# Steps 0 and 1 of a transformer tower in another order: maxima, exponentials and outputs ahead of the projections' work

## The chip, the cores and the metric

The kernel runs on one core of one Trainium2 chip. The metric is device time in microseconds (us), the median of repeated runs of the whole program. The core has five engines with their own instruction streams: PE (matrix products), DVE (vector), ACT (activation functions), POOL (GpSimd) and SP (which issues DMAs here). They meet only at semaphores, so what an engine does next is fixed by the order in which the program was written.

## The reference

It takes 16 sequences of 128 tokens and a width of 256. Cut to what matters:

```python
h = layernorm(word_emb[ids] + pos_emb + type_emb[types]) * gamma + beta
a = layernorm(h)
q, k, v = a @ Wq, a @ Wk, a @ Wv              # 16 heads of 16
q, k = layernorm(q) * qw + qb, layernorm(k) * kw + kb   # per head
h = h + softmax(causal(q @ k.T / 4)) @ v @ Wo + bo
s = softmax(layernorm(h) @ gate.T)            # 8 experts, best 2 by s + bias
h = h + sum over the 2: (silu(x w1) * (x w3)) @ w2,  x = s * layernorm(h)
```

## The kernel before, in words

The program has an attention stage, a short routing stage and an expert stage of 39 tiles of 128 rows. The change and the prediction concern the beginning of the attention stage.

**Attention** handles one sequence per step, in a software pipeline. Each engine has its own function `step(t, p, half)`, and `attention` calls it for t = -5 to 17: -5 to 2 written out, 3 to 10 in a loop of two steps, the rest written out. `valid(t)` is true for 0 to 15, and `at_step(t, n)` is true only in a step that is written out and has number n. In step t a sequence is at these places:

- Sequence t + 5: POOL gathers its word rows (`gather`, L426) and, from sequence 5 on, prepares position and type rows (L535 to L537, called x_base below).
- Sequence t + 4: DVE adds them (`sum_rows`, L888 and L892, with statistics in L775 and L776), centers them (`centered`, L899), applies the first layer norm (`first_norm`, L905) and takes statistics for the second (`stats`). POOL turns variances into reciprocal roots (`power_e`, `power_a`, L430 and L431).
- Sequence t + 3: DVE applies the second norm (`normalize_a`, L779), and POOL adds the output bias into the residual (`output_bias`, L471).
- Sequence t + 2: PE transposes the normalized rows (L1129), ACT copies them out of PSUM (L670), PE projects them to q and k (`project`, L1243), ACT squares these (`squares`, L664), DVE sums the squares per head (`squared_sums`, L862 to L865), POOL finds the reciprocal roots by ten small operations (`qk_power`, L437 to L447), and DVE multiplies (`normalize_qk`, L878).
- Sequence t + 1: PE transposes q and k (L1129), ACT copies them out with scale and bias (`queries_and_keys_out`, L657), and PE projects v (`values`).
- Sequence t: PE computes the scores (`scores`, L1202) into PSUM banks 0 to 3, into which `mask_bank` (L1194) has put the causal mask. DVE takes row maxima, one instruction per bank (`maxima`, L856). ACT takes the exponentials, four instructions per bank (`exponentials`, L620). PE transposes them (`keys_to_rows`, L1129), into the bank they came from, or into T_BANK for the last, and ACT copies the result to SBUF (`transposed`, L627).
- Sequence t - 1: PE multiplies probabilities and values (`outputs`, L1219), and ACT, PE and DVE bring the result back to rows, divide it by the sums (L983, L984) and multiply it by Wo (L1342).

T_BANK is one PSUM bank, used in turn by the transposed q and k and by the last of the four transposed banks of probabilities. The columns q and k of the next sequence must be copied out before `keys_to_rows(3)` may write there.

**Order around the change.** In the steps ahead of 0 the pipeline fills. In step 0 PE computes the scores of sequence 0, runs 14 matmuls of no use (`keep_warm`, L1137, here into T_BANK), and only then goes on. ACT takes two banks of exponentials, then copies q and k, then comes the rest. DVE takes `sum_rows(3)` and `centered(3)` at the end of step -1, then the maxima, and `normalize_qk(2)` at the end of step 0. POOL runs `power_e(4)` ahead of `qk_power(2)`. All of it waits in order: whatever stands behind a waiting instruction on an engine waits too.

At the start of the program PE runs `keep_warm(WARM_START)`, 32 matmuls of no use, until the first normalized rows are there; another 14 (`WARM_FIRST`) stand in step -1.

Of the kernel before, what the change touches and what calls it, by code (L numbers as in the profile page):

```python
# [9 lines left out]
B = 16  # L10
# [22 lines left out]
WARM_START, WARM_FIRST, WARM_EXPERTS = 32, 14, 16  # L33
# [17 lines left out]
def build_tower(nc, ids, types, word, rows, w_qkv, w_o, head_cols, gate_t, w1, w3, w2, out):  # L51
# [7 lines left out]
    with ctx:  # L59
# [311 lines left out]
        def _(pool):  # L371
# [77 lines left out]
            def step(t, p, half):  # L449
# [47 lines left out]
                else:  # L497
# [23 lines left out]
                    if valid(t + 5):  # L521
                        gather(t + 5, 1 - p, link)
                    if valid(t + 4):
                        power_e(t + 4)
                    if at_step(t, B - 3):
                        hot_cells(0, 0, 4)
                    if valid(t + 2):
                        qk_power(t + 2, link)
# [72 lines left out]
        def _(act):  # L601
# [12 lines left out]
            def step(t, p, half):  # L614
# [52 lines left out]
                if valid(u):  # L667
                    act.wait_ge(aT_ps, u + 1)
                    wait(act, v_done, u - 1)
                    a.activation(aT[p].rearrange("p k s -> p (k s)"), PS[:, O_BANK, 0:D],  # L670
                                 ACT.Copy).then_inc(aT_ready, 1)
                if valid(t):
                    exponentials(0)
                    exponentials(1)
# [72 lines left out]
        def _(dve):  # L747
# [102 lines left out]
            def step(t, p, half):  # L850
# [79 lines left out]
                elif at_step(t, -1):  # L930
                    normalize_a(2)
                    squared_sums(1)
                    sum_rows(3, 1, 1)
                    centered(3, 1)
# [5 lines left out]
                if at_step(t, 0):  # L940
                    normalize_qk(1)
                    first_norm(3)
                    stats(link, row(3), 1, var_a)
                if at_step(t, B):
                    one_hots(1, (1,))
                if at_step(t, B + 1):
                    places(2, link)
                if valid(t + 4) and valid(t):
                    sum_rows(t + 4, p, half(4))
                u = t - 2  # L950
# [35 lines left out]
                if valid(t + 2) and valid(t):  # L986
                    squared_sums(t + 2)
# [6 lines left out]
                if valid(t + 4) and valid(t):  # L994
                    first_norm(t + 4)
# [7 lines left out]
                if valid(t + 4) and valid(t):  # L1003
# [32 lines left out]
                if valid(t + 2) and valid(t):  # L1036
# [87 lines left out]
        def _(pe):  # L1124
# [55 lines left out]
            def step(t, p, half):  # L1180
# [93 lines left out]
                if at_step(t, 0):  # L1274
                    keep_warm(WARM_FIRST, T_BANK)
                u = t + 2
                if valid(u):
# [4 lines left out]
                    transposes(a_n, DK, O_BANK).then_inc(aT_ps, 1)  # L1282
                u = t + 1
# [6 lines left out]
                if valid(t - 1):  # L1290
# [12 lines left out]
                if valid(t):  # L1303
# [8 lines left out]
                if valid(t) and not at_step(t, B - 1):  # L1312
# [19 lines left out]
                if valid(t):  # L1332
# [133 lines left out]
```

## Time and profile before

| | us |
|---|---|
| median of 3 runs | 551.74 (550.8 to 553.6) |
| the profiled execution's own time | 551.53 |
| its span, first to last instruction | 549.8 |
| mean granted clock of PE in it | 0.986 of full |
| PE busy | 512.2 (93% of the span) |
| DVE, ACT, POOL busy | 285.3, 258.0, 287.2 |

The span is divided so: scores of sequence 0 start at 29.3 us, scores of sequence 15 at 200.5 us, the first expert tile's products at 232.8 us. "Busy" of an engine is time with an instruction in execution, and "idle before <-" in a row names the work that ended the idle time ahead of it. "PEclk" is the granted share of PE's full clock: 1.00 is 2.4 GHz, 0.50 is 1.2 GHz. In the timeline of PE, one matmul in the program is often two instructions, and the time of a row reaches to the end of its last one, so the next row can start up to 0.17 us before that.

### The profile page before, as it was taken

What the parts mean: (1) busy time and instruction counts of PE and PEld (TensorE: products, weight loads), DVE (VectorE), ACT (ScalarE), POOL (GpSimd) and SP (SyncE); (2) the same over time, 40 slices, a digit from 0 to 9 for tenths busy, and PEclk for the clock granted to TensorE, in tenths of its full rate; (3) what the DMA queues carried; (4) which work ended last, traced back from release to release, by engine and by line L of the source; (5) the groups of instructions that cost most, each with busy time, mean ns of one, the idle gap of its engine ahead of it and who ended that gap; (6) DMA issues with size and microseconds to landing.
All of it is one profiled execution on the core that took longest, in us unless ns stands there. A gap on an engine that the chain in (4) does not pass through costs nothing.

```text
span 549.8 us, 12957 instructions
## 1 busy us (share of the span) xinstructions
PE 512.2 (93%) x4263; PEld 432.1 (79%) x4264; DVE 285.3 (52%) x743; ACT 258.0 (47%) x591; POOL 287.2 (52%) x532
## 2 busy tenths in 40 slices
PE   6788999999999998799999999999999999999991
PEld 2345767777676765399999999999999999999981
DVE  3786888878888887723333333333333333333330
ACT  1068888988999784142333233322333223332320
POOL 4587787677754565215334544454434544454432
PEclk9899999999999999989999999999999999999996
DMA  5017611100028672401122212221122212222221
GB/s 164 10 44 270 211 49 44 44 29 29 29 76 275 212 239 81 100 20 26 36 39 39 30 28 39 39 39 23 36 39 39 33 26 38 39 34 31 32 39 19
DMA packets 29482, 36.64 MB, mean 67 GB/s; under 512 B 7792, under 2 KB 23024, under 8 KB 29456
## 3 DMA queue, kind: packets, MB, share of 16 engines
q0 software_dynamic: 8352, 12.76, 13.7%
q1 hardware_dynamic: 20288, 22.51, 12.9%
q10 hardware_dynamic: 816, 1.06, 0.6%
q8 instruction: 13, 0.21, 0.2%
q14 instruction: 13, 0.11, 0.1%
HBM read 26.81 MB, written 9.50 MB: 66 GB/s over the span
## 4 chain that ended last, share of the span: by engine, by line
PE 80%; POOL 5%; DVE 4%; ACT 4%; issue 3%; DMA 2%; SPq 0%; DVEq 0%; ACTq 0%; POOLq 0%
PE PS L1391 35%; PE PS L1402 18%; PE PS L1129 9%; PE PS L1243 6%; PE PS L1342 3%; PE PS L1202 2%; PE PS L1219 2%; PE PS L1194 2%; DMA cols_sb<-head_cols_dram 1%; ACT work L620 1%; PE PS L1256 1%; DMA out_dram<-x_pair,dst_c 1%; PE PS L1137 1%; POOL arena L471 1%; DVE ss L862 0%
## 5 line engine op out<-in xcount | busy, mean ns | idle before, releaser
L1391 PEld LDWEIGHTS PS<-work,arena 128*128 128x128 f32 x1716 | 199.2, 194 | 3.8 <-ACT work L724 2.0
L1391 PE MATMUL PS<-work,arena 128*128 128x128 f32 x1716 | 199.8, 277 | 1.5 <-ACT work L724 1.5
L730 ACT ACTIVATE work<-PS 128x768 f32<-128x768 f32 x39 | 31.6, 810 | 198.9 <-PE PS L1391 198.9
L1402 PE MATMUL PS<-w_sb,work 128*128 x468 | 107.6, 380 | 0.7 <-DVE x_pair L1104 0.7
L1096 DVE TENSOR_TENSOR work<-work,PS 128x640 f32<-128x640 f32 x39 | 32.0, 821 | 139.5 <-ACT work L730 139.5
L1402 PEld LDWEIGHTS PS<-w_sb,work 128*128 128x128 f32 x468 | 86.1, 191 | 11.0 <-issue 1.1
L564 POOL DMA_INDIRECT out_dram<-x_pair,dst_c x39 | 80.5, 2065 | 22.0 <-POOL dst_c L563 20.5
L563 POOL COPY dst_c<-dest_i 128x1 int32 (+1 forms) x39 | 7.1, 181 | 136.5 <-DVE x_pair L1104 134.3
L620 ACT ACTIVATE work<-PS,nmax 128x128 f32<-128x128 f32 x256 | 72.6, 404 | 4.7 <-DVE nmax L856 4.7
L720 ACT ACTIVATE arena<-w_sb 128x1408 f32 x40 | 55.1, 1377 | 13.9 <-DVE er_i L1072 8.9
L1129 PE MATMUL PS<-ident,work 128*128 128x128 f32 x336 | 55.4, 278 | 2.8 <-ACT work L620 1.4
L1129 PEld LDWEIGHTS PS<-ident,work 128*128 128x128 f32 x336 | 38.7, 141 | 19.8 <-ACT work L620 10.8
L1243 PE MATMUL PS<-w_sb,front 128*128 128x512 f32 (+1 forms) x128 | 48.9, 506 | 0.6 <-ACT front L670 0.6
L1082 DVE COPY arena<-w_sb 128x1408 f32 x40 | 36.0, 900 | 25.8 <-issue 25.8
L557 POOL DMA_INDIRECT work<-x_rows,src_c x39 | 39.7, 1018 | 10.8 <-POOL src_c L556 10.8
L627 ACT ACTIVATE work<-PS 128x512 f32<-128x512 f32 x64 | 42.0, 656 | 0.3 <-PE PS L1129 0.3
L856 DVE TENSOR_REDUCE nmax<-PS 128x4 f32<-128x512 f32 x64 | 39.7, 683 | 2.0 <-PE PS L1202 1.6
L1104 DVE COPY x_pair<-PS 128x256 f32<-128x256 f32 x39 | 16.6, 425 | 36.9 <-PE PS L1402 36.9
L1137 PE MATMUL PS<-identb 128*128 128x512 bf16 x115 | 29.2, 403 | 5.3 <-POOL identb L390 5.3
L556 POOL COPY src_c<-src_i 128x1 int32 (+1 forms) x39 | 29.6, 759 | 7.5 <-PE PS L1129 7.5
L1129 PE MATMUL PS<-ident,arena 128*128 128x128 f32 x160 | 25.8, 276 | 6.2 <-DVE arena L878 4.4
L1243 PEld LDWEIGHTS PS<-w_sb,front 128*128 128x128 f32 x128 | 22.0, 191 | 11.8 <-issue 10.1
(165 smaller groups left out, 621.9 us busy)
## 6 DMA issues: line engine op xcount, KB each, us to landing
w_sb<-w_dram SPq DMA_DIRECT2D x16, 640.0 KB, 6.2
w_sb<-w_dram SPq DMA_DIRECT2D x8, 704.0 KB, 4.5
x_rows<-x SPq DMA_DIRECT2D x16, 128.0 KB, 2.2
out_dram<-arena SPq DMA_DIRECT2D x16, 128.0 KB, 2.3
w_sb<-w_dram SPq DMA_DIRECT2D x16, 64.0 KB, 6.5
w_sb<-w_qkv_dram ACTq DMA_DIRECT2D x1, 768.0 KB, 8.0
work<-x_rows,src_c POOLq DMA_INDIRECT x41, 2.9
out_dram<-x_pair,dst_c POOLq DMA_INDIRECT x39, 4.2
```

What stands on the lines that cost most here:

```text
L557: g.indirect_dma_start(xg_sb[p], None, x2_dram, bass.IndirectOffsetOnAxis(src_c[p][:, :], 0)).then_inc(xg_loaded[p], 16)
L564: g.indirect_dma_start(out, bass.IndirectOffsetOnAxis(dst_c[p][:, :], 0), y_sb[p][:, :], None, compute_op=ALU.add).then_inc(y_stored[p], 16)
L620: last = a.activation(probs[:, c * P:(c + 1) * P], PS[:, r, g * P:(g + 1) * P], ACT.Exp, bias=nmax[:, c:c + 1])
L627: a.activation(probsT[:, r * 512:(r + 1) * 512], PS[:, T_BANK if r == RG - 1 else r, :], ACT.Copy).then_inc(probsT_ready, 1)
L720: a.activation(ws[p][:, 0:1, :], w13_sb[:, bass.ds(e, 1), 0, :], ACT.Copy).then_inc(w_a_ready, 1)
L856: v.tensor_reduce(nmax[:, RG * r:RG * r + RG], PS[:, r, :].rearrange("p (g s) -> p g s", s=P), axis=AX.X, op=ALU.max, negate=True).then_in ...
L1082: v.tensor_copy(ws[p][:, 1:2, :], w13_sb[:, bass.ds(e, 1), 1, :]).then_inc(w_v_ready, 1)
L1129: last = n.transpose(PS[:, bank, at + i * P:at + (i + 1) * P], src[:, i * P:(i + 1) * P], ident[:, :])
L1137: n.matmul(PS[:, bank, :], identb[:, :], spread(identb[:, :], 1, GROUPS), start=True, stop=True)
L1243: last = n.matmul(PS[:, bank, 0:w], a[:, k, :], wqkv_sb[:, k, w0:w0 + w], start=(k == 0), stop=(k == DK - 1))
L1391: last = n.matmul(up_ps[p][:, i, c, :], ws[p][:, k, at:at + P], xT_sb[p][:, k, :], start=(k == 0), stop=(k == DK - 1))
L1402: last = n.matmul(PS[:, 7, 0:D], hT_sb[p][:, i, :], w2_sb[:, bass.ds(e, 1), i, :], start=(i == 0), stop=(i == FK - 1))
```

## The change

Nothing is added to or taken from what is computed. The order of steps 0 and 1 is changed on four engines, and the number of useless matmuls in two places:

- PE: `WARM_START` is 42 instead of 32. In step 0 the 14 useless matmuls become 7, and stand behind the transposes of sequence 2's rows instead of ahead of them. `keys_to_rows(0)`, `(1)` and `(2)` of step 0 come ahead of the transposes of q and k. In step 1 `outputs(0)` comes ahead of the transposes of q and k.
- ACT: in step 0 all four exponentials come first, then two copies of probabilities, then q and k, then the rest.
- DVE: the maxima of step 0 come ahead of `sum_rows(3)` and `centered(3)`, with `normalize_qk(1)` between these two. `first_norm(4)`, its statistics and `normalize_qk(2)` move from step 0 to behind the maxima of step 1. `squared_sums(2)` moves ahead of `centered(4)`.
- POOL: `qk_power(2)` comes ahead of `power_e(4)`.

```diff
-WARM_START, WARM_FIRST, WARM_EXPERTS = 32, 14, 16
+WARM_START, WARM_FIRST, WARM_EXPERTS = 42, 14, 16
...
+                    if at_step(t, 0):
+                        qk_power(2, link)
                     if valid(t + 4):
                         power_e(t + 4)
                     if at_step(t, B - 3):
                         hot_cells(0, 0, 4)
-                    if valid(t + 2):
+                    if valid(t + 2) and not at_step(t, 0):
                         qk_power(t + 2, link)
...
+                if at_step(t, 0):
+                    for r in range(RG):
+                        exponentials(r)
+                    transposed(0)
+                    transposed(1)
+                    queries_and_keys_out(1)
+                    transposed(2)
+                    squares(2)
+                    values_out(1)
+                    transposed(3)
+                    return
...
                     squared_sums(1)
-                    sum_rows(3, 1, 1)
-                    centered(3, 1)
                 if valid(t):
                     maxima(0)
...
                 if at_step(t, 0):
+                    sum_rows(3, 1, 1)
                     normalize_qk(1)
+                    centered(3, 1)
                     first_norm(3)
                     stats(link, row(3), 1, var_a)
...
+                if at_step(t, 1):
+                    normalize_qk(2)
+                    first_norm(4)
+                    stats(link, row(4), 1, var_a)
                 if valid(t + 4) and valid(t):
                     sum_rows(t + 4, p, half(4))
+                if at_step(t, 0):
+                    squared_sums(2)
...
-                if at_step(t, 0):
-                    keep_warm(WARM_FIRST, T_BANK)
                 u = t + 2
                 if valid(u):
...
                     transposes(a_n, DK, O_BANK).then_inc(aT_ps, 1)
+                if at_step(t, 0):
+                    keep_warm(WARM_FIRST // 2, T_BANK)
+                    keys_to_rows(0)
+                    keys_to_rows(1)
+                    keys_to_rows(2)
+                if at_step(t, 1):
+                    outputs(0)
```

The calls that these replace get `and not at_step(t, 0)` (or 1) in their old places.

On PE, the stretch from the scores of sequence 0 to the last mask product of step 0 (`ident,work` rows are `keys_to_rows`, `ident,front` the transposes of normalized rows, `ident,arena` those of q and k, `w_sb,front` projections, 512 columns wide for q and k, 256 for v) stood so before:

```order
L1202 MATMUL PS<-w_sb 128x128 x16
L1137 MATMUL PS<-identb 128x512 x14
L1129 MATMUL PS<-ident,front 128x128 x2
L1129 MATMUL PS<-ident,arena 128x128 x4
L1243 MATMUL PS<-w_sb,front 128x512 x2
L1129 MATMUL PS<-ident,work 128x128 x8
L1243 MATMUL PS<-w_sb,front 128x256 x2
L1194 MATMUL PS<-mask,identb 128x512
L1129 MATMUL PS<-ident,work 128x128 x4
L1194 MATMUL PS<-mask,identb 128x512
L1129 MATMUL PS<-ident,work 128x128 x4
L1194 MATMUL PS<-mask,identb 128x512 x2
```

and stands so now:

```order
L1221 MATMUL PS<-w_sb 128x128 x16
L1148 MATMUL PS<-ident,front 128x128 x2
L1156 MATMUL PS<-identb 128x512 x7
L1148 MATMUL PS<-ident,work 128x128 x12
L1148 MATMUL PS<-ident,arena 128x128 x4
L1262 MATMUL PS<-w_sb,front 128x512 x2
L1262 MATMUL PS<-w_sb,front 128x256 x2
L1213 MATMUL PS<-mask,identb 128x512 x2
L1148 MATMUL PS<-ident,work 128x128 x4
L1213 MATMUL PS<-mask,identb 128x512 x2
L1221 MATMUL PS<-w_sb 128x128 x16
```

The useless matmuls (`identb` alone) are half as many and one place later. Twelve of the sixteen transposes of probabilities have moved from behind the projection of q and k to ahead of the transposes of q and k.

On DVE, the stretch from the end of step -1 to the statistics of sequence 3 in step 0 (`nmax` are the maxima, `arena<-PS,rqk` is `normalize_qk`, the rows from `rows_sb,typesf` to `mv<-st` are `sum_rows`, and `L269 ISA` clears a semaphore at the end of a step) stood so before:

```order
L888 SCALAR_TENSOR_TENSOR front<-rows_sb,typesf 128x256
L892 TENSOR_TENSOR x_pair<-x_pair,front 128x256
L775 BN_STATS st<-x_pair 128x6
L776 BN_AGGR mv<-st 128x2
L899 SCALAR_TENSOR_TENSOR front<-x_pair,mv,rows_sb 128x256
L269 ISA
L856 TENSOR_REDUCE nmax<-PS 128x4 x4
L878 TENSOR_TENSOR arena<-PS,rqk 128x512
L905 SCALAR_TENSOR_TENSOR arena<-front,rstd,rows_sb 128x256
L775 BN_STATS st<-arena 128x6
L776 BN_AGGR mv<-st 128x2
```

and stands so now:

```order
L269 ISA
L869 TENSOR_REDUCE nmax<-PS 128x4 x4
L901 SCALAR_TENSOR_TENSOR front<-rows_sb,typesf 128x256
L905 TENSOR_TENSOR x_pair<-x_pair,front 128x256
L788 BN_STATS st<-x_pair 128x6
L789 BN_AGGR mv<-st 128x2
L891 TENSOR_TENSOR arena<-PS,rqk 128x512
L912 SCALAR_TENSOR_TENSOR front<-x_pair,mv,rows_sb 128x256
L918 SCALAR_TENSOR_TENSOR arena<-front,rstd,rows_sb 128x256
L788 BN_STATS st<-arena 128x6
L789 BN_AGGR mv<-st 128x2
```

The maxima have moved ahead of the four instructions of `sum_rows(3)`, and `centered(3)` (L899, L912 now) to behind `normalize_qk(1)`.

## Rows read from the trace of the kernel before

**Rows 1.** the page, section 4: the chain that ended last, shares of the span
```profile
PE 80%; POOL 5%; DVE 4%; ACT 4%; issue 3%; DMA 2%; SPq 0%; DVEq 0%; ACTq 0%; POOLq 0%
```

**Rows 2.** windows, one step each: length, busy by engine, granted clock, DMA share, GB/s
```profile
29.30:43.37 14.07, 10.75 (x82) 6.41 (x81) 12.39 (x29) 9.49 (x28) 11.81 (x29) 1.00 0.31 103
...
55.51:66.59 11.08, 10.84 (x115) 7.95 (x114) 8.93 (x24) 9.77 (x30) 8.07 (x21) 1.00 0.54 175
```

**Rows 3.** timeline of PE: start us, us, engine, line, operation, [idle before <-releaser]
```profile
5.31 8.58 PE L1137 MATMUL PS<-identb 128*128 128x512 bf16 x32 [5.31 <-POOL identb L390]
...
17.73 2.94 PE L1243 MATMUL PS<-w_sb,front 128*128 128x512 f32 x4 [0.56 <-ACT front L670]
...
20.46 3.97 PE L1137 MATMUL PS<-identb 128*128 128x512 bf16 x14
...
27.49 1.88 PE L1243 MATMUL PS<-w_sb,front 128*128 128x512 f32 x4
...
30.41 3.20 PE L1137 MATMUL PS<-identb 128*128 128x512 bf16 x14
```

**Rows 4.** windows, clock after the warm start, and two stretches of little PE work
```profile
19.00:20.00 1.00, 1.00 (x2) 0.50 0.13 49
...
13.89:17.73 3.84, 0.41 (x3) 0.21 (x3) 3.63 (x10) 0.38 (x1) 2.50 (x4) 1.00 0.00 0
...
33.82:36.75 2.93, 0.50 (x5) 0.50 (x5) 2.93 (x5) 2.44 (x9) 2.60 (x8) 1.00 0.00 0
```

**Rows 5.** timeline of DVE, from the first squared sums to step 1
```profile
21.33 0.69 DVE L862 TENSOR_REDUCE ss<-w_sb 128x32 f32<-128x512 f32 x1 [0.93 <-ACT w_sb L664]
...
31.07 0.48 DVE L888 SCALAR_TENSOR_TENSOR front<-rows_sb,typesf 128x256 f32<-128x256 f32 x1
...
33.12 2.48 DVE L856 TENSOR_REDUCE nmax<-PS 128x4 f32<-128x512 f32 x4
...
35.51 0.68 DVE L878 TENSOR_TENSOR arena<-PS,rqk 128x512 f32<-128x512 f32 x1
...
45.91 2.48 DVE L856 TENSOR_REDUCE nmax<-PS 128x4 f32<-128x512 f32 x4
```

**Rows 6.** timeline of ACT, step 1: exponentials
```profile
46.62 2.17 ACT L620 ACTIVATE work<-PS,nmax 128x128 f32<-128x128 f32 x8 [1.29 <-DVE nmax L856]
```

**Rows 7.** timeline of PE, steps 0, 1 and 2
```profile
36.25 0.66 PE L1129 MATMUL PS<-ident,arena 128*128 128x128 f32 x4 [2.43 <-DVE arena L878]
...
36.75 1.88 PE L1243 MATMUL PS<-w_sb,front 128*128 128x512 f32 x4
...
42.35 0.66 PE L1129 MATMUL PS<-ident,work 128*128 128x128 f32 x4 [0.64 <-ACT work L620]
...
46.05 0.66 PE L1129 MATMUL PS<-ident,arena 128*128 128x128 f32 x4 [1.14 <-DVE arena L878]
...
56.89 0.60 PE L1129 MATMUL PS<-ident,arena 128*128 128x128 f32 x4
```

**Rows 8.** timeline of POOL, steps -1 to 1
```profile
34.95 0.19 POOL L430 TENSOR_TENSOR veps<-mv,eps 128x1 f32<-128x1 f32 x1
...
35.76 2.27 POOL L471 TENSOR_TENSOR arena<-arena,rows_sb 128x256 f32<-128x256 f32 x3
...
37.99 0.37 POOL L430 TENSOR_TENSOR veps<-mv,eps 128x1 f32<-128x1 f32 x1
...
41.79 0.23 POOL L437 TENSOR_TENSOR nwt<-guess 128x32 f32<-128x32 f32 x1
...
47.20 0.73 POOL L537 TENSOR_TENSOR front<-front,rows_sb 128x256 f32<-128x256 f32 x1
...
52.37 0.41 POOL L437 TENSOR_TENSOR nwt<-guess 128x32 f32<-128x32 f32 x1 [1.26 <-DVE guess L865]
...
55.65 0.25 POOL L447 TENSOR_TENSOR rqk<-nwt 128x32 f32<-128x32 f32 x1
```

**Rows 9.** windows, from DVE's sum of sequence 5 to squared sums of sequence 3
```profile
48.30:52.28 3.98, 3.94 (x23) 2.63 (x21) 3.20 (x11) 3.98 (x12) 2.41 (x5) 1.00 0.59 170
```

More of the change, by code:

```diff
@@ L985, in step @@
                                     spread(rden[:, :], 2, HD), ALU.mult).then_inc(o_ready, 1)
-                if valid(t + 2) and valid(t):
+                if valid(t + 2) and valid(t) and not at_step(t, 0):
                     squared_sums(t + 2)
@@ L993, in step @@
                     choose(2, link)
-                if valid(t + 4) and valid(t):
+                if valid(t + 4) and valid(t) and not at_step(t, 0):
                     first_norm(t + 4)
@@ L1002, in step @@
                     normalize_a(t + 3)
-                if valid(t + 4) and valid(t):
+                if valid(t + 4) and valid(t) and not at_step(t, 0):
                     stats(link, row(t + 4), 1, var_a)
@@ L1035, in step @@
                     stats(link, row(u), 2, var_f)
-                if valid(t + 2) and valid(t):
+                if valid(t + 2) and valid(t) and not at_step(t, 0):
                     normalize_qk(t + 2)
@@ L1289, in step @@
                     transposes(qkn, 2 * DK, T_BANK).then_inc(qk_ps, 1)
-                if valid(t - 1):
+                if valid(t - 1) and not at_step(t, 1):
                     outputs(t - 1)
@@ L1302, in step @@
                     project(u, aT[p], QK_BANK, 0, 2 * D, qk_done)
-                if valid(t):
+                if valid(t) and not at_step(t, 0):
                     keys_to_rows(0)
@@ L1311, in step @@
                     outputs_back(t - 1)
-                if valid(t) and not at_step(t, B - 1):
+                if valid(t) and not at_step(t, 0) and not at_step(t, B - 1):
                     keys_to_rows(1)
@@ L1331, in step @@
                     mask_bank(t + 1, 0)
-                if valid(t):
+                if valid(t) and not at_step(t, 0):
                     keys_to_rows(2)
```

## The prediction

> **What bounds the kernel.** I read the chain that ended last first: PE makes 80% of it, DVE, ACT and POOL 13% together [rows 1]. Next the windows of single steps, since a share of the whole says nothing of steps 0 and 1. A settled step, from scores(2) to scores(3), takes 11.08 us with PE busy in 10.84 of them; step 0 takes 14.07 us, with PE busy in 10.75, and step 1 takes 55.51 - 43.37 = 12.14 us [rows 2]. So the change has 2.99 + 1.06 = 4.05 us to work on there, and its warm start acts before that. From scores(2) on PE has work almost without a gap, so what is won by then should last. Last came the timelines, for which wait ends last.
>
> **The warm start.** Thirty-two matmuls last 8.58 us; the first projection to q and k then takes 2.94 us, where the second takes 1.88 [rows 3]. The granted clock is 0.50 (1.2 GHz) meanwhile, after 3.84 us in which PE was busy for 0.41 [rows 4]. Those 0.41 are the transposes of the first normalized rows. Ten more matmuls at the mean of the first row last 2.7 us and end near 16.6, and with the transposes PE is then idle for 0.7 us of what was a stretch of 3.84. If the clock holds, the projection ends 2.94 - 1.88 = 1.06 us earlier. DVE's squared sums follow it directly, but had waited only 0.93 us [rows 5]; before that DVE was at work. So the chain through `qk_power(0)`, the transposes of q and k, the second projection and scores(0) moves by **0.93 us**, and scores(0) goes from 29.30 to 28.37. The 14 useless matmuls of step -1 (3.97 us, partly at the low clock, against 3.20 in step 0 [rows 3]) end well ahead of the q and k that PE waits for there.
>
> **Step 0.** Below, times of the trace are moved by this 0.93. Without `sum_rows(3)` and `centered(3)`, which held DVE from 31.07 to 33.12 [rows 5], the maxima start at 31.07 - 0.93 = 30.1; scores(0) are done by 28.37 + 1.2. Exponentials start 0.71 us after the maxima do (45.91 to 46.62), and eight take 2.17 [rows 5, 6]. All 16 end near 30.1 + 0.7 + 4.3 = 35.1, the first twelve near 34.1, and their transposes, 0.66 us for a set of four [rows 7], at 34.8. DVE needs 35.51 - 33.12 = 2.39 for the maxima [rows 5], and for the four instructions put between, four of the five that filled those 2.05, some 1.65: `normalize_qk(1)` starts at 34.2 instead of 35.51. PE takes its transposes 0.74 us later (35.51 to 36.25), at 34.9, just behind the transposed probabilities. This is 1.3 us early, of which only 0.4 is due to the order.
>
> The larger gain is behind it. Before, 6.62 us passed from the projection of q and k, at 36.75 [rows 7], to scores(1), at 43.37 [rows 2]. Now the path holds that projection, 1.88 less the overlap of 0.16, so 1.72; the values, half as wide, 0.86; two mask products, of the form of the useless matmuls and so 3.20 / 14 = 0.23 each [rows 3]; then the last bank and two masks, 43.37 - 42.35 = 1.02: 4.06 us. Twelve transposes and the waits for exponentials, the last of them 0.64 [rows 7], have left it. Scores(1) start at 34.9 + 0.5 + 4.06 = 39.4, **3.9 us early**. ACT must have copied q and k of sequence 1 by then: behind the exponentials and two copies it starts at 36.1 and ends at 37.6, so this holds.
>
> **Steps 1 and 2: what is late next.** The chain through POOL. From `power_e(3)` at 34.95 to the end of `qk_power(3)` at 55.90, POOL has 20.95 us with one wait of note, 1.26 us for the squared sums of sequence 3 [rows 8]. This list of work is the same afterwards, since `power_e(4)` and `qk_power(2)` only change places. It now starts at 34.35, when DVE has the statistics of sequence 3. Going through it: `power_e(4)` ended at 41.79 [rows 8], so `qk_power(2)`, now ahead of that (0.81 us, as `power_e(3)`, from 34.95 to 35.76), starts at 41.79 - 0.60 - 0.81 = 40.4. At the 55.90 - 52.37 = 3.5 us of `qk_power(3)` it ends at 43.9. Its q and k reach PE at 44.7 instead of 46.05 [rows 7]. PE has done outputs(0) by then and stands for some 2 us. Then the prepared rows of sequence 5 are late. POOL's x_base(5) was done at 47.20 + 0.73 = 47.93 [rows 8], and is now at 47.3; DVE, which comes to it some 1.5 us sooner, waits. And `sum_rows(5)` stands ahead of the division for sequence 0 and the squared sums of sequence 3. These took 3.98 us together, with DVE busy in 3.20 [rows 9]; without the wait for PE I take 3.4, so they end at 50.7. POOL comes free at 52.37 - 1.26 - 0.60 = 50.5. Of its 1.26 us of wait 0.2 is left.
>
> `qk_power(3)` then ends at 55.90 - 0.60 - 1.06 = 54.2, and PE can take those q and k at 55.0. Before, PE took them at 56.89 [rows 7], when it had time. So **1.9 us** of the 3.9 last, and PE waits there for about 0.5 us. From here both kernels have the same order and the shift stays. I take off 0.1, for one stretched item of POOL.
>
> **The sum.** 0.93 from the warm start and 0.9 from the order: 1.8 us. The profiled execution took 551.53, so 549.7; the median of before is 0.2 above it, so **549.9**. That is 0.33%; a measurement of this kernel tells about 0.5% (2.8 us) from no change.
>
> **The unknown price** is how long POOL's list takes beside a DVE without gaps. The same small instruction took 0.19 us at 34.95 and 0.37 at 37.99 [rows 8], so its items stretch. If the list grows by a twentieth, 1.0 us, 0.8 of the gain is left; if the stretches of before do not recur, it shrinks by 0.7 and the gain is 2.5. I take it unchanged, since the list ran beside a DVE busy in 12.39 of 14.07 us already [rows 2], and keep both ends.
>
> **Rivals.**
> - *POOL does not hold the order back (13%).* If its list is shorter, or the q and k of sequence 3 are not what PE waits for, 3.8 us last: 547.9. For it speaks that PE is the chain's main engine [rows 1]; against it, that POOL has only 1.26 us of slack in 20.95 [rows 8].
> - *The warm start buys nothing (12%).* The clock falls all the same at the first projection, or DVE is no earlier: 549.9 + 0.9 = 550.8. For it: 3.84 us with 0.41 of work led to a fall; against it: 2.93 us with 0.50 did not [rows 4], and the new stretch is shorter.
> - *The clock falls in step 0 or 1 (20%).* With 7 useless matmuls PE does nothing but transposes from 31.2 to 35.4, and stands for 2 us in step 1. A low spell costs 1.06 for one projection, and with the matmuls behind it (3.97 against 3.20 [rows 3]) 1.8: 551.0 to 551.7. The 2.93 us [rows 4] held only transposes and the tail of a matmul, and the clock stood. The Trainium skill (TensorE: Matmul & The Clock Gate, Part 4: PE-mode transpose) says that transposes do not count as busy for the clock in the same way. By this rule 4.2 us would count as idle, longer than the 3.84 that led to a fall, and this rival would be the forecast, at 551.4. The one row that bears on it speaks against it, but was shorter, so it keeps a fifth.
> - *Slower (5%).* The clock falls in both places and PE, not POOL, is the bound there, so each low spell costs its 1.8 in full: 549.9 + 3.6 = 553.5. It is slower than before from 1.8 us lost, that is from the second spell on.
>
> **How the numbers follow.** The forecast has 50%. The range holds it with its bounds (gain 0.8 to 2.5: 549.2 to 550.9), the weak warm start and the single fall, and is drawn out to 548.2 for a part of the first rival and to 551.8. It leaves out most of the first rival and the last. Faster by over 0.5%, below 549.0: the first rival and 5 points of the forecast, 18%. Slower by over 0.5%, above 554.5: a tail of the last rival and what I do not see, 4%. Between, 78%.
>
> **What would show it.** The first projection takes 1.9 us at clock 1.00; scores(0) start at 28.4, the maxima of step 0 at 30.1, scores(1) near 39.4. In step 1 PE waits about 2 us for DVE's `normalize_qk(2)`, DVE waits for x_base(5), and POOL works from 34.4 to 54 with under 0.5 us of waits. Scores(2) start near 53, PE takes q and k of sequence 3 near 55, and scores(3) start at 64.8 instead of 66.59. I am wrong if scores(3) are early by 3 us or more, or by less than 0.8, or if the clock shows a spell of 0.50 between 31 and 50 us.

## The result and the profile after

Over 17 runs of each, the changed kernel takes 549.01 us (547.73 to 551.73) and the kernel before 550.76 us (548.75 to 553.6). The ratio is 0.9967, with a 95% interval of 0.9952 to 0.9981: 1.8 us faster, 0.33%, and by the bound of 0.5%, which the prediction set, no change. The forecast was 549.9 with a gain of 1.8. The level is lower than forecast because the kernel before had its median at 550.76 in the larger set, not at 551.74.

The page, sections 1 and 4, against [rows 1]:

```profile
PE 510.8 (94%) x4266; PEld 430.8 (79%) x4267; DVE 286.0 (52%) x743; ACT 258.2 (47%) x591; POOL 287.4 (53%) x532
...
PE 81%; POOL 6%; DVE 4%; issue 3%; ACT 3%; DMA 1%; DVEq 0%; POOLq 0%; ACTq 0%
```

PE is the bound as it was. The windows of steps 0, 1 and 2, against [rows 2] (length, busy time of PE, PEld, DVE, ACT and POOL, granted clock, DMA share, GB/s):

```profile
28.65:39.56 10.91, 9.49 (x74) 5.79 (x73) 10.21 (x22) 9.39 (x28) 8.75 (x22) 1.00 0.10 28
39.56:52.55 12.99, 10.22 (x110) 7.31 (x109) 10.48 (x27) 9.78 (x29) 11.09 (x28) 1.00 0.81 272
52.55:64.76 12.21, 11.17 (x116) 7.90 (x115) 9.40 (x25) 9.82 (x30) 9.29 (x27) 1.00 0.66 204
```

Step 0 has shrunk from 14.07 to 10.91 us. Step 1 has grown from 12.14 to 12.99 and step 2 from 11.08 to 12.21: of the 3.16 us that step 0 won, 1.98 are given back. The timeline of PE, against [rows 3] and [rows 7]:

```profile
5.29 11.96 PE L1156 MATMUL PS<-identb 128*128 128x512 bf16 x42 [5.29 <-POOL identb L390]
...
17.09 0.38 PE L1148 MATMUL PS<-ident,front 128*128 128x128 f32 x2
...
18.02 1.99 PE L1262 MATMUL PS<-w_sb,front 128*128 128x512 f32 x4 [0.56 <-ACT front L672]
...
28.65 1.17 PE L1221 MATMUL PS<-w_sb 32*128 32x128 f32 x32
...
35.10 0.66 PE L1148 MATMUL PS<-ident,arena 128*128 128x128 f32 x4
...
41.82 1.08 PE L1238 MATMUL PS<-work,front 128*32 128x128 f32 x32 [0.56 <-ACT front L672]
...
44.33 0.66 PE L1148 MATMUL PS<-ident,arena 128*128 128x128 f32 x4 [1.44 <-DVE arena L891]
...
49.58 0.44 PE L1148 MATMUL PS<-ident,arena 128*128 128x128 f32 x2 [0.70 <-DVE arena L1003]
...
55.02 0.66 PE L1148 MATMUL PS<-ident,arena 128*128 128x128 f32 x4 [0.93 <-DVE arena L891]
...
64.76 1.17 PE L1221 MATMUL PS<-w_sb 32*128 32x128 f32 x32
```

PE waits 0.56 us ahead of outputs(0), 1.44 ahead of the q and k of sequence 2, 0.70 ahead of the divided outputs of sequence 0 (L1003), and 0.93 ahead of the q and k of sequence 3, the last three for DVE. The timeline of DVE, against [rows 5]:

```profile
30.44 2.49 DVE L869 TENSOR_REDUCE nmax<-PS 128x4 f32<-128x512 f32 x4
...
34.37 0.67 DVE L891 TENSOR_TENSOR arena<-PS,rqk 128x512 f32<-128x512 f32 x1
...
47.27 0.43 DVE L905 TENSOR_TENSOR x_pair<-x_pair,front 128x256 f32<-128x256 f32 x1 [1.26 <-POOL front L539]
```

The last of these is `sum_rows(5)`, which waits 1.26 us for POOL's x_base(5). The timeline of POOL, against [rows 8]:

```profile
34.53 0.19 POOL L430 TENSOR_TENSOR veps<-mv,eps 128x1 f32<-128x1 f32 x1 [0.35 <-DVE mv L789]
...
40.34 0.23 POOL L437 TENSOR_TENSOR nwt<-guess 128x32 f32<-128x32 f32 x1
...
46.51 0.73 POOL L539 TENSOR_TENSOR front<-front,rows_sb 128x256 f32<-128x256 f32 x1
...
50.74 0.23 POOL L437 TENSOR_TENSOR nwt<-guess 128x32 f32<-128x32 f32 x1
...
53.99 0.25 POOL L447 TENSOR_TENSOR rqk<-nwt 128x32 f32<-128x32 f32 x1
```

The wait of 1.26 us ahead of `qk_power(3)` is gone: none stands at 50.74, and POOL works from 34.53 to 54.24 with no wait of note.

The span fell by 3.6 us (549.8 to 546.2), twice the gain of the medians. The rest is another thing. The first expert tile's 44 products, in the timeline of PE, before:

```profile
232.80 6.81 PE L1391 MATMUL PS<-work,arena 128*128 128x128 f32 x44 [0.53 <-ACT work L724]
```

and after:

```profile
230.90 5.18 PE L1415 MATMUL PS<-work,arena 128*128 128x128 f32 x44 [0.53 <-ACT work L737]
```

In the profiled execution of before the clock had fallen there (0.50 from 234 to 237 us), in that of after it had not. These 1.63 us belong to the two executions: this place of the program is the same in both, and 6.81 and 5.18 us are both found there in kernels with the new order. Comparisons of one execution with another are therefore made at the start of scores(3), at 66.59 and 64.76, ahead of that place.

### The profile page after: what moved, and what is told of

Same layout as the page of the kernel before. It is cut to its first block, busy times and chain, and to the rows that moved or that the text cites. A ratio compares the mean times of both kernels' runs of the same rounds, so it can differ in the third digit from the quotient of the medians.

```text
span 546.2 us, 12963 instructions
## 1 busy us (share of the span) xinstructions
PE 510.8 (94%) x4266; PEld 430.8 (79%) x4267; DVE 286.0 (52%) x743; ACT 258.2 (47%) x591; POOL 287.4 (53%) x532
## 4 chain that ended last, share of the span: by engine, by line
PE 81%; POOL 6%; DVE 4%; issue 3%; ACT 3%; DMA 1%; DVEq 0%; POOLq 0%; ACTq 0%
PE PS L1415 35%; PE PS L1426 18%; PE PS L1148 9%; PE PS L1262 6%; PE PS L1156 3%; PE PS L1366 2%; PE PS L1238 2%; PE PS L1221 2%; PE PS L1213 2%; PE PS L1275 1%; ACT work L622 1%; DVE nmax L869 1%; POOL arena L471 1%; DMA out_dram<-x_pair,dst_c 1%; POOL x_pair L426 1%
## 5 line engine op out<-in xcount | busy, mean ns | idle before, releaser
L1262 PE MATMUL PS<-w_sb,front 128*128 128x512 f32 (+1 forms) x128 | 47.7, 497 | 0.6 <-ACT front L672 0.6
L1123 DVE COPY x_pair<-PS 128x256 f32<-128x256 f32 x39 | 16.6, 425 | 36.9 <-PE PS L1426 36.9
L1156 PE MATMUL PS<-identb 128*128 128x512 bf16 x118 | 30.3, 407 | 5.3 <-POOL identb L390 5.3
```

Of the source, the lines that this page charges most:

```text
L1156: n.matmul(PS[:, bank, :], identb[:, :], spread(identb[:, :], 1, GROUPS), start=True, stop=True)
L1262: last = n.matmul(PS[:, bank, 0:w], a[:, k, :], wqkv_sb[:, k, w0:w0 + w], start=(k == 0), stop=(k == DK - 1))
```

## The experiments

The theory: POOL's list from `power_e(3)` to `qk_power(3)` decides what is kept of the early start, and the longer warm start adds a microsecond of its own. There are two rivals: that POOL does not matter and PE's own work decides (the "PE theory" of the expectations), and that the clock, not the order, makes the difference.

Executions differ by some tenths of a microsecond in when the first gathered rows arrive. So the table counts from the start of DVE's first sum of gathered rows (10.43 us in the span of before, 10.52 in that of after). "List" is the start of `power_e(3)` on POOL; the last column is the stretch of clock 0.50 before 60 us, in time of the span. Each row is one profiled execution, so a difference in the last column can be one between executions.

| kernel | scores(0) | scores(1) | list | scores(2) | scores(3) | clock low |
|---|---|---|---|---|---|---|
| before | 18.87 | 32.94 | 24.52 | 45.08 | 56.16 | 18.6 to 22.0 |
| changed | 18.13 | 29.04 | 24.01 | 42.03 | 54.24 | none |
| order alone | 17.80 | 28.92 | 23.89 | 41.93 | 54.17 | none |
| warm start alone | 17.81 | 33.52 | 23.45 | 44.40 | 55.48 | 36.1 to 39.5 |
| x_base(5) on DVE | 17.82 | 28.94 | 23.91 | 41.10 | 53.26 | none |
| POOL 1 us longer | 17.81 | 28.93 | 23.90 | 42.93 | 55.14 | none |
| no useless matmuls in step 0 | 18.29 | 30.66 | 24.18 | 42.83 | 55.06 | 34.4 to 37.8 |
| outputs(0) back | 18.10 | 29.02 | 23.99 | 43.97 | 55.76 | 44.4 to 47.8 |
| POOL's order back | 17.85 | 28.77 | 23.74 | 44.52 | 56.41 | 43.6 to 50.5 |
| sum_rows(3) first | 18.08 | 30.29 | 23.50 | 43.31 | 55.54 | none |
| outputs(0) back, matmuls | 18.31 | 29.44 | 24.40 | 42.83 | 54.70 | none |
| outputs(0) back, transposes | 17.81 | 28.88 | 23.84 | 42.27 | 54.13 | none |
| POOL's order back, matmuls | 17.81 | 28.92 | 23.88 | 41.90 | 53.97 | none |
| combined | 17.82 | 28.95 | 23.91 | 41.14 | 53.33 | none |

### The two halves: the order alone, the warm start alone

```diff
-WARM_START, WARM_FIRST, WARM_EXPERTS = 42, 14, 16
+WARM_START, WARM_FIRST, WARM_EXPERTS = 32, 14, 16
```

> 

> The changed kernel with the 32 useless matmuls of before at the start, so the new order alone. Two theories. POOL theory: after step 1 what is kept of the gain is set by POOL's list of work from power_e(3) to qk_power(3), which runs almost without a wait. Rival, PE theory: PE's own work sets it, and POOL has slack. On this kernel both expect the start of scores(0) as in the kernel before, 29.3 us. The first projection takes 2.9 us again at a granted clock of 0.50. Scores(1) start 3.1 to 3.3 us earlier than before (40.2), scores(3) at 65.4, which is 1.2 us earlier than before and 0.65 later than with the change. If the warm start were what the gain of the change comes from, scores(3) would start at 66.6.

In the kernel before, the same line the other way round:

> 

> The kernel before with 42 instead of 32 useless matmuls at the start, nothing else. The first projection takes 1.9 to 2.0 us at clock 1.00. Scores(0) start at 28.65 as with the change, 0.65 us earlier than before, and all later scores too: scores(3) at 65.9. Together with the run of the order alone this tells whether the two parts add up to the 1.85 us of the whole change. A rival: where POOL's list binds, the 0.65 is partly lost, and scores(3) start at 66.2 or later.

Measured: 550.79 us for the order alone, ratio 0.9978 (0.9952 to 1.0004), and 550.14 for the warm start alone, ratio 0.9975 (0.9955 to 0.9995). The timeline of PE with the order alone, up to its first projection:

```profile
16.88 0.41 PE L1148 MATMUL PS<-ident,front 128*128 128x128 f32 x2 [2.39 <-DVE front L792]
17.84 1.98 PE L1262 MATMUL PS<-w_sb,front 128*128 128x512 f32 x4 [0.56 <-ACT front L672]
```

The expectation missed here. With 32 useless matmuls the clock did not fall at the first projection this time (1.98 us, not 2.94), though the program is the same up to there. The 32 took 9.12 us in this execution, not 8.58, so PE was idle for 2.39 us behind them and not for 2.88; whether that decided it, one profile of each can't tell. The order without that fall has the same scores(3) as the whole change, 54.17 against 54.24. So in these two profiles, where the clock holds at the first projection in both, the ten matmuls more gained nothing. Of the 1.92 us between the two profiles of before and after, about half may be the clock at the first projection. This is an estimate from the 1.07 us by which scores(0) are earlier with the order alone (17.80 against 18.87); there is no profile of before without that fall. With the warm start alone, the window of PE (length, busy time, clock, DMA share, GB/s):

```profile
36.00:38.00 2.00, 2.00 (x5) 0.53 0.00 0
```

and in its timeline:

```profile
35.53 0.66 PE L1129 MATMUL PS<-ident,arena 128*128 128x128 f32 x4 [2.43 <-DVE arena L878]
...
36.02 3.51 PE L1243 MATMUL PS<-w_sb,front 128*128 128x512 f32 x4
```

The clock fell in step 0, behind a wait of 2.43 us. The same wait, of the same length, stands in the profile of before [rows 7], and there the clock stayed at 1.00 [rows 4]. The projections took 3.51 us instead of 1.88, and scores(1) were late. By scores(3) most of that was made up, 55.48 against 56.16 in before, 0.68 us early. So whether the halves add up can't be checked from two single profiles with falls in different places. The ratios, 0.22% and 0.25% faster with intervals of 0.2% and more either way, neither add up to 0.33% nor contradict it.

### POOL's list: 2 us off, 1 us on

x_base(5) is taken from POOL, where it is three instructions of step 0, and given to DVE as one in step 1:

```diff
-        EARLY = 5
+        EARLY = 6
...
-                    if valid(u):
+                    if valid(u) and not (isinstance(u, int) and u < EARLY):
```

> 

> The changed kernel, with x_base(5) computed by one DVE instruction in step 1 and not by three on POOL in step 0. POOL's list is shorter by 2.0 us, DVE's longer by 0.5. POOL theory: qk_power(3) starts 1.4 us earlier (at 49.3, when DVE has the squared sums), PE takes q and k of sequence 3 at 53.7 to 53.9 instead of 55.0, and scores(3) start 1.1 to 1.4 us earlier, at 63.4 to 63.7; the time falls by about as much. PE theory: nothing changes, scores(3) at 64.8, or they are later by the 0.5 us on DVE.

And one instruction of it is done twice:

```diff
                         link(g.tensor_scalar(x_base, type_diff, tcol[:, :], None, ALU.mult))
+                        if at_step(t, 0):
+                            link(g.tensor_scalar(x_base, type_diff, tcol[:, :], None, ALU.mult))
```

> 

> The changed kernel with one of POOL's instructions for x_base(5) done twice (in step 0 alone), 1.0 us more on POOL. POOL theory: scores(3) start 1.0 us later, at 65.8, and PE's wait for q and k of sequence 3 grows from 0.9 to about 1.9 us. PE theory: POOL has slack, and scores(3) stay within 0.2 of 64.8.

Scores(3) with x_base(5) on DVE, and then PE's waits and scores(3) with POOL 1 us longer:

```profile
63.58 1.17 PE L1221 MATMUL PS<-w_sb 32*128 32x128 f32 x32
```

and

```profile
50.76 0.44 PE L1150 MATMUL PS<-ident,arena 128*128 128x128 f32 x2 [1.71 <-DVE arena L1005]
...
56.20 0.66 PE L1150 MATMUL PS<-ident,arena 128*128 128x128 f32 x4 [0.93 <-DVE arena L893]
...
65.94 1.17 PE L1223 MATMUL PS<-w_sb 32*128 32x128 f32 x32
```

Both starts are where the POOL theory has them. From DVE's first sum they are 53.26 and 55.14, with the same start of scores(0) and of the list as the order alone has (54.17): 0.91 us earlier and 0.97 later. One microsecond on POOL is one microsecond on PE at scores(3). But one part of that expectation missed: PE's wait for the q and k of sequence 3 did not grow to 1.9 us, it is 0.93 as with the change. PE had lost the microsecond already in step 1, ahead of the divided outputs (1.71 us of wait, with the change 0.70), and scores(2) were 1.0 us later than with the order alone (42.93 against 41.93). The way from POOL to PE is first the late x_base(5), which holds DVE's `sum_rows(5)` and all that stands behind it, and only then the end of the list. Two off give only 0.9, since POOL then waits for DVE, as its timeline shows for `power_a(4)`:

```profile
45.79 0.34 POOL L430 TENSOR_TENSOR veps<-mv,eps 128x1 f32<-128x1 f32 x1 [1.05 <-DVE mv L789]
```

The times: 548.75 us, ratio 0.9933 (0.991 to 0.9955), and 549.53, ratio 0.9947 (0.9927 to 0.9967). By its ratio the second is not slower than the change, and its interval overlaps that of the change. The medians of 4 and 6 executions don't resolve a microsecond, so this result rests on the timelines alone, one of each kernel.

### Parts of the order undone

outputs(0) stands in its old place in step 1:

```diff
-                if at_step(t, 1):
-                    outputs(0)
...
-                if valid(t - 1) and not at_step(t, 1):
+                if valid(t - 1):
                     outputs(t - 1)
```

> 

> The changed kernel with outputs(0) behind the transposes of q and k again in step 1. POOL theory: PE waits there anyway, so q and k of sequence 2 are transposed at 44.3 as before, everything behind on PE is up to 1.0 us later, scores(2) start at 53.3 to 53.6 instead of 52.55, but the division of sequence 0 still waits for x_base(5), so scores(3) start at 64.8 to 65.0: this part of the change buys nothing that lasts. PE theory: scores(3) are later by the full 1.0 us, 65.8.

`power_e(4)` is ahead of `qk_power(2)` again:

```diff
-                    if at_step(t, 0):
-                        qk_power(2, link)
                     if valid(t + 4):
                         power_e(t + 4)
...
-                    if valid(t + 2) and not at_step(t, 0):
+                    if valid(t + 2):
                         qk_power(t + 2, link)
```

> 

> The changed kernel with power_e(4) ahead of qk_power(2) on POOL again. POOL theory: the list is as long as it was, so q and k of sequence 2 reach PE 0.8 us later (45.1), scores(2) start near 53.3, but qk_power(3) ends at 54.2 as with the change and scores(3) start at 64.8 to 65.0. PE theory: scores(3) later by 0.8 us, 65.5.

Both expectations failed: scores(3) came 1.5 and 2.2 us later than with the change, where neither theory had more than 1.0. PE with outputs(0) back, its timeline and two windows of 2 us (length, busy time, clock, DMA share, GB/s):

```profile
44.04 0.84 PE L1148 MATMUL PS<-ident,arena 128*128 128x128 f32 x4 [3.08 <-DVE arena L891]
```

```profile
44.00:46.00 2.00, 1.96 (x28) 0.60 0.95 308
46.00:48.00 2.00, 2.00 (x18) 0.55 0.05 13
```

and the same two views with POOL's order back:

```profile
44.63 1.11 PE L1146 MATMUL PS<-ident,arena 128*128 128x128 f32 x4 [2.27 <-DVE arena L889]
...
45.54 3.62 PE L1260 MATMUL PS<-w_sb,front 128*128 128x512 f32 x4
```

```profile
44.00:46.00 2.00, 1.37 (x5) 0.50 0.79 271
46.00:48.00 2.00, 2.00 (x3) 0.50 0.07 18
```

PE stood for 3.08 and for 2.27 us. The clock went to 0.50 (1.2 GHz) just behind the wait in the first (from 44.4 to 47.8) and within the wait in the second (from 43.6 to 50.5). The slow projection makes the squared sums of sequence 3 late, and POOL stands again ahead of `qk_power(3)`, 1.49 us in the first kernel and 2.51 in the second, here in its timeline of POOL:

```profile
52.59 0.41 POOL L437 TENSOR_TENSOR nwt<-guess 128x32 f32<-128x32 f32 x1 [2.51 <-DVE guess L876]
```

In the changed kernel PE's wait at this place is 1.44 us, and the clock stays. So these parts may matter by the clock and not by the order. To tell the two apart, PE's wait was filled with useless matmuls in the same two kernels, 12 in the first and 9 in the second:

```diff
+                    if at_step(t, 1):
+                        pe.wait_ge(v_ready, 2)
+                        keep_warm(12, VY_BANK)
                     pe.wait_ge(qkn_ready, u + 1)
```

> 

> As the run with outputs(0) behind the transposes of q and k, with 12 useless matmuls in the place where PE waits 3.08 us for them in step 1 (from 40.8 to 43.4), so that the clock has no cause to fall. That run's scores(3) were 1.5 us later than with the change, and its clock was at 0.50 from 44.4 to 47.8. If the delay came from the fall of the clock, no stretch of 0.50 is seen, scores(2) start 0.7 to 1.0 us later than with the change and scores(3) at 54.2 to 54.4 us after DVE's first sum, as with the change (54.24). If the delay came from the order itself, scores(3) are 1 us or more later still, 55.2 or more after that sum.

> 

> As the run with power_e(4) ahead of qk_power(2), with 9 useless matmuls in the place where PE waits 2.27 us for q and k in step 1. That run's scores(3) were 2.2 us later than with the change, with the clock at 0.50 from 43.8 to 50.6. If the fall of the clock made the delay, no stretch of 0.50 is seen and scores(3) start 54.2 to 54.4 us after DVE's first sum (POOL's list is as long). If the order made it, 55.0 or more.

The timeline of PE with outputs(0) back and 12 matmuls:

```profile
44.43 0.66 PE L1148 MATMUL PS<-ident,arena 128*128 128x128 f32 x4 [0.50 <-DVE arena L891]
...
64.91 1.17 PE L1221 MATMUL PS<-w_sb 32*128 32x128 f32 x32
```

and with POOL's order back and 9 matmuls:

```profile
45.47 0.66 PE L1146 MATMUL PS<-ident,arena 128*128 128x128 f32 x4 [0.22 <-DVE arena L889]
...
64.92 1.17 PE L1219 MATMUL PS<-w_sb 32*128 32x128 f32 x32
```

The clock stays at 1.00 in both, and scores(3) start at 54.70 and 53.97. The first is 0.46 later than with the change, but its list on POOL began 0.39 later too (24.40 against 24.01), before the place where the two differ. The second is 0.27 earlier. So in these profiles the order of outputs(0) and of POOL's two items has no lasting effect of its own; what was lost in the first two kernels is the clock. The four kernels were executed once each (549.33 us and 550.14 with the parts undone, 549.78 and 550.04 with the matmuls), so their times show nothing, and how often the clock falls in them is not known.

`sum_rows(3)` ahead of the maxima again:

```diff
                     squared_sums(1)
+                    sum_rows(3, 1, 1)
...
                 if at_step(t, 0):
-                    sum_rows(3, 1, 1)
                     normalize_qk(1)
```

> 

> The changed kernel with sum_rows(3) ahead of the maxima of step 0 again, centered(3) staying behind. The maxima and all exponentials are 1.65 us later, and POOL's list starts 0.3 us earlier. POOL theory: the transposed probabilities now hold PE, scores(1) start at 41.0, the squared sums of sequence 2 come too late for POOL (41.4 instead of 40.1), POOL waits some 1.2 us for them, and scores(3) start 1 us later than with the change, at 65.6 to 66.0. If early maxima buy nothing that lasts: 64.8.

Its timeline of POOL:

```profile
41.30 0.40 POOL L437 TENSOR_TENSOR nwt<-guess 128x32 f32<-128x32 f32 x1 [1.31 <-DVE guess L878]
```

POOL waits 1.31 us for the squared sums of sequence 2, where 1.2 was expected, and scores(3) start at 65.91 (55.54 from the first sum), 1.3 us later than with the change, with no fall of the clock (one execution, of 549.3 us). This is the part of the order whose effect lasts by itself: early maxima bring early exponentials, and these the projection of sequence 2 and its squares, in time for POOL.

### The clock in step 0, and whether transposes keep it up

The 7 useless matmuls of step 0 are left out:

```diff
                 if at_step(t, 0):
-                    keep_warm(WARM_FIRST // 2, T_BANK)
                     keys_to_rows(0)
```

> 

> The changed kernel without the 7 useless matmuls of step 0: between the transposes of sequence 2's rows (30.0 us) and the projection for sequence 2 (35.6) PE runs nothing but 16 transposes. Theory A, transposes do not count as work for the clock: 5.6 us without any other work, longer than the 3.84 us after which the clock fell in the kernel before, so the granted clock is 0.50 for some 3.4 us from 34 to 37 on, the projection takes 2.7 us or more, scores(1) start at 40.4 or later, and the mean clock of the executions is lower by about 0.003 than with the change (median 0.989). Theory B, they count: no stretch of 0.50, scores(1) at 39.6, and the same clocks and times as with the change.

Its timeline of PE, and the window behind:

```profile
32.21 0.66 PE L1148 MATMUL PS<-ident,work 128*128 128x128 f32 x4 [2.17 <-ACT work L622]
...
35.95 3.67 PE L1262 MATMUL PS<-w_sb,front 128*128 128x512 f32 x8
```

```profile
34.00:36.00 2.00, 1.73 (x9) 0.60 0.00 0
```

The clock falls in step 0, the two projections take 3.67 us instead of 2.75, scores(1) start at 40.86, and scores(3) 0.8 us later than with the change. The median is 550.01, ratio 0.9983 (0.9961 to 1.0006), an interval that overlaps that of the change, and the median clock of ten executions is 0.986 (0.989 with the change). This is what theory A (transposes do not keep the clock up) expected, but it doesn't prove it, since PE also stood still for 2.17 us there before the first transposes. With `sum_rows(3)` first it stood for as long, with the 7 matmuls ahead of the wait, and the clock stayed at 1.00 through 5.2 us with only transposes and waits, as the timeline of PE in that kernel shows:

```profile
33.69 0.66 PE L1148 MATMUL PS<-ident,work 128*128 128x128 f32 x4 [2.19 <-ACT work L622]
```

The direct test puts 24 useless transposes where 12 useless matmuls had kept the clock up:

```diff
-                        keep_warm(12, VY_BANK)
+                        for _ in range(6):
+                            for i in range(GROUPS):
+                                n.transpose(PS[:, VY_BANK, i * P:(i + 1) * P], ident[:, :], ident[:, :])
```

> 

> As the run with 12 useless matmuls in step 1 (no fall of the clock, scores(3) 54.70 us after DVE's first sum), with 24 useless transposes of the same length in their place. Theory A, transposes do not count as work for the clock: it falls as in the run with nothing there, a stretch of 0.50 begins between 43 and 47 us, scores(3) start 55.4 or more after that sum, and the mean clock of the executions lies by 0.003 below that with the change (median 0.989). Theory B, they count: no stretch of 0.50 there, scores(3) at 54.2 to 54.7, clocks as with the change. The step 0 of ten profiles so far speaks for B: 3.9 to 5.2 us with nothing but transposes, and no fall.

Its timeline of PE, and two of its windows (length, busy time, clock, DMA share, GB/s):

```profile
41.07 2.78 PE L1312 MATMUL PS<-ident 128*128 128x128 f32 x24
...
44.34 0.65 PE L1148 MATMUL PS<-ident,arena 128*128 128x128 f32 x4 [0.48 <-DVE arena L891]
...
45.93 1.98 PE L1262 MATMUL PS<-w_sb,front 128*128 128x512 f32 x4
```

```profile
43.00:44.00 1.00, 0.86 (x8) 1.00 1.08 364
46.00:47.00 1.00, 1.00 (x4) 1.00 0.29 72
```

The clock is 1.00 throughout, the next projection takes 1.98 us, and scores(3) start at 54.13. That agrees with theory B, by which transposes keep the clock up as matmuls do. It takes 549.42 us, ratio 0.9967 (0.9946 to 0.9987), and the median clock of ten executions is 0.990, where theory A expected 0.986. Where nothing stood in that place, the clock fell, but in the only execution there is of that kernel. So it is shown that 24 transposes did not bring the clock down here; that they, and not the execution, kept it up is likely and not proven.

### x_base(5) on DVE, with other numbers of useless matmuls

The changed kernel gets x_base(5) on DVE, two useless matmuls fewer at the start, and four more ahead of the first expert tile:

```diff
-WARM_START, WARM_FIRST, WARM_EXPERTS = 42, 14, 16
+WARM_START, WARM_FIRST, WARM_EXPERTS = 40, 14, 20
...
-        EARLY = 5
+        EARLY = 6
...
-                    if valid(u):
+                    if valid(u) and not (isinstance(u, int) and u < EARLY):
```

> 

> The changed kernel with x_base(5) on DVE, 40 instead of 42 useless matmuls at the start and 20 instead of 16 ahead of the experts (where the clock fell before the first tile's products in the profiles of before, of the order alone and of two others, which then took 6.81 and not 5.18 us). POOL theory: scores(3) start 53.0 to 53.3 us after DVE's first sum (54.24 with the change, 53.26 with x_base(5) on DVE alone). Clock: the first tile's products take 5.18 us. The median falls by 1.0 us from POOL and by up to 1.6 where the clock fell: 547.0 to 548.0 in executions where before takes 551, a ratio of 0.992 to 0.994. If neither holds, it is as the change, 0.997.

Its timeline of PE, scores(3) and the first tile:

```profile
64.31 1.17 PE L1221 MATMUL PS<-w_sb 32*128 32x128 f32 x32
...
230.66 5.18 PE L1415 MATMUL PS<-work,arena 128*128 128x128 f32 x44 [0.53 <-ACT work L737]
```

It takes 547.84 us (546.7 to 548.97, 11 runs), ratio 0.9935 (0.9917 to 0.9954). Scores(3) start 53.33 after the first sum, as with x_base(5) on DVE alone, and the first tile takes 5.18 us. The interval overlaps that of the change by 0.0002 only, and the median is 1.2 us below it. It has the lowest median of the study, but its ratio is that of x_base(5) on DVE alone, 0.9933: the 20 matmuls ahead of the experts show no gain beside it in the times, though the first tile took 6.81 us in that kernel's profile and 5.18 in this one. The median clock is 0.992 here, and 0.989 in the four executions with x_base(5) on DVE alone, which is too few to say that the fall is cured. The two useless matmuls fewer show nothing: scores(0) start at 17.82 with 40 and, in five of the kernels with 42, at 17.81 or 17.82.

## Why the prediction was right, and where its steps were off

- **The warm start: the step that was off.** At scores(0) 0.93 us were forecast and 0.65 measured (28.65 against 29.30). The first projection took 1.99 us instead of 2.94. But the term had a second price that I had left out: 42 matmuls took 11.96 us, not 8.58 + 2.7 = 11.3, and the transposes of the first rows started at 17.09 instead of 16.77. The step by which they "end near 16.6", ahead of those transposes, failed by 0.5 us. I had also taken the fall in before for a property of the program. The order alone, with 32 matmuls, ran without it and had scores(3) at the same place as the whole change (54.17 and 54.24). So the split of the forecast into 0.93 for the warm start and 0.9 for the order is not confirmed by any run: what the ten matmuls gain depends on whether a fall would have come, and how often that is isn't known.
- **Step 0: right.** Maxima at 30.44 (forecast 30.1), transposes of q and k at 35.10 (34.9), scores(1) at 39.56 (39.4), 3.81 us early (3.9).
- **POOL's list: right, link by link.** `power_e(3)` at 34.53 (34.35), `qk_power(2)` at 40.34 (40.4), x_base(5) done at 47.24 (47.3), squared sums of sequence 3 done at 50.55 (50.7), `qk_power(3)` done at 54.24 (54.2), q and k of sequence 3 on PE at 55.02 (55.0), scores(3) at 64.76 (64.8). That POOL's work sets this, and not PE's, the two runs with POOL's work changed show: 0.97 us for 1.0 added, 0.91 for 2.0 taken away.
- **PE's waits: in part.** I had 2 us ahead of the q and k of sequence 2, where it was 1.44 behind a first wait of 0.56, and 0.5 ahead of those of sequence 3, where it was 0.93. PE was ahead by more than I had counted (scores(2) at 52.55, not 53), and waited for the same POOL. A third wait, 0.70 us for the divided outputs, was in the text as the lateness of x_base(5) and not as a wait of PE; it is where the microsecond added to POOL showed first.
- **The rival "POOL does not hold the order back"** fell with the loaded and the relieved list.
- **The rival "the warm start buys nothing"** is not settled. The clock held at the first projection and scores(0) were earlier, by 0.65 us, but the order alone did as well with 32 matmuls. The median of before with 42, 550.14 us, is too near to the others to tell.
- **The rival "slower"** didn't come. No profile had a fall both in step 0 and in step 1.
- **The rival "the clock falls in step 0 or 1"** didn't come in the profile of the change, but three of its near relations show how close it is: without the 7 matmuls, without outputs(0) in its new place, or with POOL's old order the clock fell in the one profile taken of each. The reason the text gave for it, that transposes do not count as busy for the clock in the same way (the Trainium skill, TensorE: Matmul & The Clock Gate, Part 4: PE-mode transpose), isn't borne out here. The clock held over twenty-four f32 transposes as over twelve matmuls, and 3.9 us with only transposes and short waits, in step 0, never led to a fall in any profile of a kernel with the 7 matmuls.
- **What two parts of the change are for** was not in the sum. With `qk_power(2)` or outputs(0) in its old place PE waited 2.3 or 3.1 us in step 1, and with both in the new ones 1.44 us. I had seen that PE had done outputs(0) by then, and had priced neither place by the clock. This guards the gain and is no gain over the kernel before, which waits 1.14 us there [rows 7] at clock 1.00.
- **The agreement of the two gains, 1.8 forecast and 1.75 measured, is closer than the reasoning deserves.** The executions of before alone spread over 4.9 us, and the interval of the ratio goes from 1.0 to 2.6 us. At scores(3) the two profiles are 1.83 us apart, but about half of this may be the fall at the first projection, which a profile of before need not have.

What stays open: how often the clock falls at each place. Over 62 executions of the kernel before and the 17 of the change the mean clock and the span are known, not the place. Of before, 13 had a mean clock above 0.9905 and a median span of 547.5 us, 10 one below 0.9825 and a median span of 551.5. Of the change 8 had one above 0.9905, at a median of 546.3, and none one below 0.984. Among executions with a clock above 0.9905 the change is 1.2 us faster.

## What to carry to other kernels

When steps that fill a pipeline are reordered, walk the list of the helper engine that has the fewest waits, item by item: the time at which it ends bounds what is kept of a gain on the main engine, and a microsecond added to it was 0.97 us at scores(3). Fill a wait of PE with work that is due anyway, even if that work is not late: in step 1 the clock stayed with 1.4 us of wait and fell with 2.3 and 3.1, in one execution each. No limit follows from this, since in step 0 a wait of 2.43 us ended in a fall in one profile and not in another. And compare places in two timelines, not two spans: one fall of the clock somewhere else (1.6 us here) is as large as the whole change.

## What the runs showed of the hardware that was not expected

- The same stretch of the program was met with a fall of the clock in some profiles and without one in others. In step 0, a wait of 2.43 us with the same work around it was followed by clock 0.50 with the warm start alone and by 1.00 in before. Ahead of the first tile's products, where PE waits 1.19 and 0.53 us with two transposes between, 6.81 us were measured in before and in five of the other profiles, and 5.18 in the rest.
- The spread of the times goes with the mean granted clock: 547.5 us of span above 0.9905 and 551.5 below 0.9825, for one kernel.
- The clock stayed at 1.00 over 24 transposes (2.78 us) in the place where it fell without them, one profile of each.
- The useless matmuls at the start take a varying time: 42 of them 10.89 to 11.96 us, 32 of them 8.58 and 9.12.
